# A one-layer attention and feed-forward kernel: the opening re-ordered, loads by need, both value projections moved into the first head's steps 1 and 2

## What is computed

```python
def attention(x, wq, wk, wv, wo):
    q, k, v = heads(x @ wq), heads(x @ wk), heads(x @ wv)      # 32, 8, 8 heads of 128
    q = q * cos + rotate_half(q) * sin
    k = k * cos + rotate_half(k) * sin
    scores = q @ k.T / sqrt(128), masked to keys <= query      # k, v shared by 4 query heads
    return merge(softmax(scores) @ v) @ wo

x = layernorm(x + attention(x, wq, wk, wv, wo))
nx = x * rsqrt(mean(x * x) + 1e-5) * ln_w
x = layernorm(x + (silu(nx @ gate.T) * (nx @ up.T)) @ down.T)
```

## Time and profile before

| | us |
|---|---|
| median of 3 runs | 1170.01 |
| lowest, highest run | 1169.91, 5764.48 |
| profiled execution | 1172.84 |
| its span (first to last instruction) | 1171.0 |
| PE busy | 1119.6 (96%) |
| POOL busy | 820.7 (70%) |
| DVE busy | 802.8 (69%) |
| ACT busy | 620.2 (53%) |

### The profile page before, as it was taken

How to read it: one execution, slowest core, us unless ns; L and a number is a source line. 1 busy time by engine, 2 the same in 40 slices (tenths; PEclk the granted TensorE clock), 3 DMA queues, 4 the chain that set the end, 5 groups by cost and what they waited for, 6 DMA issues and landing times.

```text
span 1171.0 us, 18940 instructions
## 1 busy us (share of the span) xinstructions
PE 1119.6 (96%) x5346; PEld 942.4 (80%) x5346; DVE 802.8 (69%) x1416; ACT 620.2 (53%) x1122; POOL 820.7 (70%) x543
## 2 busy tenths in 40 slices
PE   7799999999999999999999999999997799999997
PEld 6678888887888788878888887888775588888885
DVE  5688788778777887788788877777888742222224
ACT  4556666666666566565666566666654342212224
POOL 3489978996898789789978996898774343333431
PEclk9899999999999999999999999999999899999999
DMA  5766555555554666466555655555455301111101
GB/s 187 190 154 154 141 139 136 151 125 142 134 145 124 146 159 157 120 153 158 150 129 147 152 125 135 149 143 125 126 139 134 106 19 53 54 54 54 54 0 72
DMA packets 148346, 144.56 MB, mean 123 GB/s; under 512 B 15200, under 2 KB 128864, under 8 KB 148320
## 3 DMA queue, kind: packets, MB, share of 16 engines
q1 hardware_dynamic: 136160, 124.31, 41.3%
q10 hardware_dynamic: 12160, 19.93, 6.2%
HBM read 37.23 MB, written 2.10 MB: 34 GB/s over the span
## 4 chain that ended last, share of the span: by engine, by line
PE 62%; POOL 16%; issue 10%; DMA 4%; DVE 3%; ACT 2%; SPq 1%; ACTq 0%; POOLq 0%; DVEq 0%
PE ACC L1064 13%; PE ACC L1066 13%; PE ACC L1065 13%; PE S L1064 4%; PE S L1066 4%; PE S L1065 4%; POOL PT_lo L499 4%; POOL qk_raw L473 4%; PE S L1080 3%; PE S L1082 3%; PE S L1081 3%; POOL rope_s L474 3%; POOL Q_lo L483 2%; DMA rope_s<-qk_raw 2%; POOL wq_lo L453 2%
## 5 line engine op out<-in xcount | busy, mean ns | idle before, releaser
L803 DVE CUSTOM_DVE_ANT_0 S<-S,mask 128x128 f32<-128x128 f32 (+7 forms) x256 | 194.4, 759 | 155.0 <-PE S L1082 155.0
L593 ACT ACTIVATE probs<-S,neg_max 128x128 f32<-128x128 f32 (+7 forms) x256 | 189.2, 739 | 207.4 <-DVE neg_max L803 204.9
L499 POOL TENSOR_TENSOR PT_lo<-PT_lo,PT_hi 128x896 fp32r<-128x896 f32 (+1 forms) x97 | 218.3, 2250 | 36.2 <-ACT PT_hi L600 36.1
L814 DVE STREAM_TRANSPOSE turned<-probs 128x128 f32<-128x128 f32 (+7 forms) x256 | 197.8, 773 | 4.0 <-ACT probs L593 4.0
L874 DVE SCALAR_TENSOR_TENSOR y<-ACC,row_rcp,y 128x512 f32<-128x512 f32 x256 | 177.2, 731 | 16.6 <-PE ACC L1066 16.6
L473 POOL TENSOR_TENSOR qk_raw<-qk_raw,cos_sb 128x512 f32<-128x512 f32 x76 | 116.9, 1538 | 97.2 <-DMA rope_s<-qk_raw 97.1
L600 ACT ACTIVATE PT_hi<-PT_lo 128x896 fp32r<-128x896 f32 (+3 forms) x160 | 162.3, 1015 | 29.6 <-DMA PT_lo<-turned 29.2
L551 POOL TENSOR_TENSOR PT_lo<-rope_s,PT_hi 128x512 fp32r<-128x512 f32 x28 | 36.3, 1297 | 156.9 <-ACT PT_hi L742 156.9
L1064 PE MATMUL ACC<-PT_hi,V_hi 128*128 128x512 f32 (+3 forms) x384 | 134.2, 349 | 7.0 <-DVE PT_lo L821 4.4
L1080 PE MATMUL S<-K_hi,Q_hi 128*128 (+5 forms) x384 | 133.3, 347 | 7.4 <-ACT probs L593 5.0
L1065 PE MATMUL ACC<-PT_lo,V_hi 128*128 128x512 f32 (+3 forms) x384 | 134.9, 351 | 0.0
(11 more groups left out here) (129 smaller groups left out, 2552.0 us busy)
## 6 DMA issues: line engine op xcount, KB each, us to landing
PT_lo<-turned SPq DMA_DIRECT2D x256, 112.0 KB, 2.5
PT_lo<-turned SPq DMA_DIRECT2D x128, 208.0 KB, 4.0
rope_s<-qk_raw ACTq DMA_DIRECT2D x152, 128.0 KB, 3.8
PT_lo<-turned SPq DMA_DIRECT2D x128, 128.0 KB, 2.6
PT_lo<-turned SPq DMA_DIRECT2D x128, 80.0 KB, 2.3
wq_raw<-in_L_attn_wq_dram SPq DMA_DIRECT2D x32, 256.0 KB, 3.0
wo_raw<-in_L_attn_wo_dram SPq DMA_DIRECT2D x32, 256.0 KB, 3.7
turned<-in_L_ffn_gate_w_t_dram SPq DMA_DIRECT2D x7, 512.0 KB, 3.9
```

Source lines behind the costliest of these rows:

```text
L499: nc.gpsimd.tensor_tensor(lo, lo.bitcast(F32), hi.bitcast(F32), ALU.subtract).then_inc(pt_lo_done[half], 1)
L593: nc.scalar.activation(dst, src, ACT.Exp, bias=neg_max[:, at:at + 1], scale=-1.0, accum_out=row_sum[:, j % 2, i:i + 1]).then_inc(exp_done, 1)
L803: nc.vector.tensor_tensor_reduce(src, src, bias, scale=1.0, scalar=MASKED, op0=ALU.add, op1=ALU.min, accum_out=neg_max[:, at:at + 1]).then ...
L814: nc.vector.transpose(dst.rearrange("p b (r i) -> p r b i", i=QB), src.rearrange("p (r b i) -> p r b i", b=4, i=QB)).then_inc(turn_done, 1)
```

## The change

All of it lies in the first head and what comes ahead of it; the loops over the later heads keep their instructions.

- Both value projections leave `START` and become the extras of steps (0,1) and (0,2).
- The tables are loaded in halves: the cosine half ahead of the second half of transposed x, the sine half behind it, the two later halves after the second rotation. wk has a semaphore of its own. wv goes into `wo_raw`, issued after the first rotation, and waits for no buffer; the first wo follows it. The plain x comes in four pieces of 512 KB ahead of steps 1 to 4.
- ACT now makes the high part of wk, wv and the second wq; DVE makes the low part of wk, POOL those of wv and the second wq.
- DVE's list: key weights' low part, then a wait for both first table halves, the cosine product of q half 0, the four low parts of x's second half, and the rest of the rotations interleaved; the last two low parts and the last sum come after steps 0 and 1. ACT's list is interleaved likewise: the first copy comes ahead of the split of x's second half.
- On POOL, in steps 4 and 5 of the first head, the low part of the rotated query comes ahead of that of the probabilities.

```diff
-    if i == 0 and j + 1 < heads:
+    if j == 0 and i in V_FIRST:
+        return [V_FIRST[i] + (0, 0, NC)]
+    if i == (0 if j else 0) and j + 1 < heads:
         return [("q", 0, j + 1, 0, NC)]
...
-START = [("q", 0), ("k", 0), ("q", 1), ("k", 1), ("v", 0), ("v", 1)]
+START = [("q", 0), ("k", 0), ("q", 1), ("k", 1)]
+V_FIRST = {1: ("v", 0), 2: ("v", 1)}
...
                 if (half, begin) == (1, 0):
-                    sp.dma_start(wkv_raw[:], wk_v[:, :, 0:HD]).then_inc(wkv_in, 16)
+                    sp.dma_start(wkv_raw[:], wk_v[:, :, 0:HD]).then_inc(first_wk_in, 16)
+                    sp.dma_start(cos_sb[:, 0:HALF], cos_t[:, 0:HALF]).then_inc(table_in[0], 16)
...
-            sp.dma_start(cos_sb[:], cos_t).then_inc(cos_in, 16)
-            sp.dma_start(sin_sb[:], sin_t).then_inc(sin_in, 16)
-            sp.wait_ge(wkv_done, 1)
-            sp.dma_start(wkv_raw[:], wv_v[:, :, 0:HD]).then_inc(wkv_in, 16)
+            sp.dma_start(sin_sb[:, 0:HALF], sin_t[:, 0:HALF]).then_inc(table_in[0], 16)
...
+            rotate()
+            sp.dma_start(flat(wo_raw).rearrange("p (c n) -> p c n", n=HD), wv_v[:, :, 0:HD]).then_inc(first_wv_in, 16)
+            rotate()
+            for table, source in ((cos_sb, cos_t), (sin_sb, sin_t)):
+                sp.dma_start(table[:, HALF:T], source[:, HALF:T]).then_inc(table_in[1], 16)
+            load_wq(1)
+            rotate()
+            rotate()
             sp.wait_ge(xt_lo_done, 2 * NC)
-            sp.dma_start(y[:], x_v).then_inc(x_in, 16)
             for j, i in FIRST_HEAD:
                 if i == 1:
+                    load_wq(2)
+                if i == 0:
+                    sp.wait_ge(wkv_done, 2)
                     load_wo(0, None)
+                if i in (1, 2, 3, 4):
+                    rows = slice(i * 2 - 2, i * 2)
+                    sp.dma_start(y[:, rows, :], x_v[:, rows, :]).then_inc(x_in, 16)
...
+            for part in range(3):
+                xT_raw_high(part)
+            act_e.wait_ge(first_wk_in, 16)
+            nc.scalar.activation(wkv_hi[:], wkv_raw[:], ACT.Copy).then_inc(w_hi_done, 1)
+            copy_out("q", 0, start=True)
+            xT_raw_high(3)
+            xT_raw_high(4)
+            copy_out("k", 0, start=True)
+            start_high(0)
+            copy_out("q", 1, start=True)
+            act_e.wait_ge(first_wv_in, 16)
+            nc.scalar.activation(wo_hi[:, 1], flat(wo_raw), ACT.Copy).then_inc(w_hi_done, 1)
+            start_high(1)
+            copy_out("k", 1, start=True)
+            act_e.wait_ge(wq_in, 32)
+            nc.scalar.activation(wq_hi[:], wq_raw[:], ACT.Copy).then_inc(w_hi_done, 1)
             exponent(0, 0)
-            start_high(3, 0)
+            start_high(2)
...
             for j, i in FIRST_HEAD:
                 step(j, i, 0)
+                if i == 0:
+                    start_high(3)
...
+            xT_raw_low(0, 0, NC)
+            dve.wait_ge(w_hi_done, 2)
+            nc.vector.tensor_tensor(wkv_lo[:], wkv_raw[:], wkv_hi[:].bitcast(F32), ALU.subtract).then_inc(wkv_done, 1)
             dve.wait_ge(const_done, 7)
-            dve.wait_ge(cos_in, 16)
-            dve.wait_ge(sin_in, 16)
-            for k in range(3):
-                start_rope(k)
-            start_rope(3, meanwhile=lambda: maximum(0))
-            start_low(3)
+            dve.wait_ge(table_in[0], 32)
+            start_cos(0)
+            xT_raw_low(1, 0, NC)
+            start_sum(0)
+            start_cos(1)
+            start_low(0)
+            start_sum(1)
+            dve.wait_ge(table_in[1], 32)
+            start_cos(2)
+            start_low(1)
+            start_sum(2)
+            maximum(0)
+            start_cos(3)
...
             for j, i in FIRST_HEAD:
                 step(j, i)
-            dve.wait_ge(x_in, 16)
+                if i == 0:
+                    start_low(2)
+                    start_sum(3)
+                if i == 1:
+                    start_low(3)
+            dve.wait_ge(x_in, 16 * HT)
```

More of the change, by code:

```diff
@@ L259, in layer_kernel @@
         x_in, x_t_in = sem("x_in"), [sem(f"x_t_in{part}") for part in range(len(X_PARTS))]
-        cos_in, sin_in, ln_w_in = sem("cos_in"), sem("sin_in"), sem("ln_w_in")
+        table_in, ln_w_in = [sem(f"table_in{h}") for h in range(2)], sem("ln_w_in")
         wq_in, wkv_in, wo_in = sem("wq_in"), sem("wkv_in"), sem("wo_in")
+        first_wk_in, first_wv_in = sem("first_wk_in"), sem("first_wv_in")
         gate_in, up_in, down_in = sem("gate_in"), sem("up_in"), sem("down_in")
@@ L454, in split, with split_wq, split_wkv, split_first_wv @@
                 n.add(kind)
[L456 to L462, removed]
+            def split_wq():
+                split("wq", flat(wq_raw), flat(wq_hi), flat(wq_lo), wq_done)
+            def split_wkv():
+                split("wkv", flat(wkv_raw), flat(wkv_hi), flat(wkv_lo), wkv_done)
+            def split_first_wv():
+                split("wkv", flat(wo_raw), wo_hi[:, 1], wo_lo[:, 1], wkv_done)
             def split_wo():
                 slot = n.n["wo"] % 2
-                split("wo", flat(wo_raw), wo_hi[:, slot], wo_lo[:, slot], wo_in, wo_done)
+                split("wo", flat(wo_raw), wo_hi[:, slot], wo_lo[:, slot], wo_done)
             def rope_sum(half, ago):
@@ L504, in step @@
                     split_wo()
-                if i in (4, 5):
+                if i in (4, 5) and j > 0:
                     pt_low(i - 4)
@@ L514, in step @@
                     rope_low(*qk_halves(kind, half, head, k_slot), later)
+                if i in (4, 5) and j == 0:
+                    pt_low(i - 4)
                 if i == 6 and not (last and j >= REP - 2):
@@ L523, in _ @@
             n.add("wq")
-            split_wkv(both=True)
-            split_wkv(first=True, both=True)
+            n.add("wkv")
+            pool.wait_ge(wkv_done, 1)
+            split_first_wv()
             pool.wait_ge(x_done, 3)
-            split_wq(both=True)
-            pool.wait_ge(cos_in, 16)
-            pool.wait_ge(sin_in, 16)
+            split_wq()
+            for half in range(2):
+                pool.wait_ge(table_in[half], 32)
             pool.wait_ge(rope_lo_done, 4)
@@ L603, in weight_hi, with rope_high @@
             def weight_hi(kind, hi, raw, arrived):
-                act_e.wait_ge(arrived, n[kind] * 16 + 16)
+                act_e.wait_ge(arrived, (n[kind] - (2 if kind == "wkv" else 0)) * 16 + 16)
                 nc.scalar.activation(hi, raw, ACT.Copy).then_inc(w_hi_done, 1)
                 n.add(kind)
-            def rope_high(hi, ago=0, summed=qk_raw):
+            def rope_high(hi, ago=0):
                 act_e.wait_ge(rope_sum_done, n["rope"] - ago)
-                nc.scalar.activation(hi, summed[:, (n.n["rope"] - 1 - ago) % 2], ACT.Copy).then_inc(rope_hi_done, 1)
+                nc.scalar.activation(hi, qk_raw[:, (n.n["rope"] - 1 - ago) % 2], ACT.Copy).then_inc(rope_hi_done, 1)
             def copy_out(kind, half, start=False):
@@ L684, in _, with xT_raw_high @@
             nc.scalar.activation(wq_hi[:], wq_raw[:], ACT.Copy).then_inc(w_hi_done, 1)
-            for arrived, (half, begin, end) in zip(x_t_in, X_PARTS):
-                act_e.wait_ge(arrived, 16)
+            def xT_raw_high(part):
+                half, begin, end = X_PARTS[part]
+                act_e.wait_ge(x_t_in[part], 16)
                 for c in range(begin, end):
@@ L689, in _, with start_high @@
                     nc.scalar.activation(xT_hi[:, c, cols], xT_raw[:, c, cols], ACT.Copy).then_inc(xt_hi_done, 1)
-            def start_high(u, ago):
+            def start_high(u):
                 kind, half = START[u]
                 cols = slice(half * HALF, (half + 1) * HALF)
[L695 to L700, removed]
+                act_e.wait_ge(rope_sum_done, u + 1)
+                nc.scalar.activation(Q_hi[:, cols] if kind == "q" else K_hi[:, 0, cols], start_c[:, u % 2],
+                                     ACT.Copy).then_inc(rope_hi_done, 1)
+            for part in range(3):
[14 more added lines that the diff above has]
+            nc.scalar.activation(wq_hi[:], wq_raw[:], ACT.Copy).then_inc(w_hi_done, 1)
             exponent(0, 0)
-            start_high(3, 0)
+            start_high(2)
             n.add("wq", 2)
@@ L830, in start_low, with start_cos @@
                 nc.vector.tensor_tensor(lo, start_c[:, k % 2], hi.bitcast(F32), ALU.subtract).then_inc(rope_lo_done, 1)
-            def start_rope(k, meanwhile=None):
+            def start_cos(k):
                 half, r = START[k][1], k % 2
-                cols = slice(half * HALF, (half + 1) * HALF)
                 dve.wait_ge(copy_done, k + 1)
@@ L899, in _, with xT_raw_low @@
             nc.vector.tensor_tensor(wq_lo[:], wq_raw[:], wq_hi[:].bitcast(F32), ALU.subtract).then_inc(wq_done, 1)
-            for half in range(2):
-                for c in range(NC):
+            nc.vector.memset(eps_rms[:], RMS_EPS * LN_EPS).then_inc(y_free, ADDS_BEFORE)
```

(4 more changed lines are left out.)

26 lines of the change are left out of this document (7 added, 19 removed).

## The result

The changed kernel takes 1167.68 us (median of 9 runs, 1164.93 to 1168.83), the kernel before 1170.01 (9 runs, one of them the disturbed one). The ratio is 0.9975 with a 95% interval of 0.9965 to 0.9985: 2.9 us faster by the ratio, 2.3 by the medians, against a forecast of 2.2. The profiled execution took 1166.82 us with a span of 1165.0.

The account below looks back on a forecast made before the run. PE was taken as the bound behind 63.92 us, keeping any shift of the opening. Tile 4 of the second head at 61.7 instead of 63.92 gave 2.2 us: 1170.0 - 2.2 = 1167.8 us, range 1164.2 to 1170.4.

Parts of the forecast that it names:

- T4: Tile 4 of the second head, the opening's last wait of PE; forecast to start at 61.7 us instead of 63.92.
- The sine half, the new wait: DVE waits for the sine table's first half, landing at 14.45 us, ahead of four low parts; key-weight gain lost.
- DVE's chain to the first score: DVE's work from sine half to first score, 9.65 us; first score at 24.1 instead of 28.62, 4.5 us earlier.
- The second wq: Weights for the next query projection, split by ACT then POOL (1.26 to 1.6 us), ready at 26.2 us.
- The clock: PE's clock falls once around the next query's projection: 3.4 us at half rate, 1.7 us lost.
- Rival A: The clock doesn't fall: everything from 26.3 us is 1.7 us earlier, tile 4 at 60.0, time 1166.1; chance 0.25.
- From 26.3 to the second copy: PE works 10.3 plus 1.7 us to 38.3; then DVE, parcel and ACT put the next query's second copy at 46.4.
- From the copy to T4: Second copy of the next query to tile 4 of the second head: the same 15.2 us as before.
- C: Clock falls a second time, between row tiles' end and tile 4 of the second head: 1.7 us lost, 1169.5; chance 0.10.
- D: DVE's wait for a late sine half passes through to tile 4; landing at 18 us gives 1171.3; chance 0.08.
- E: No effect: second swap still lands at 55.1 us, late by the parcels beside it; 1170 us; chance 0.08.
- F: Larger gain: second swap and parcels land 2 to 3 us sooner, or DVE and POOL hinder less; 1164; chance 0.09.

Follow-up runs that it names:

- the run with the gap filled: Changed kernel plus five idle identity matmuls, four ahead of the first score and one behind tile 1's scores; 1166.01 us, ratio 0.9966.
- the kernel with the values alone: Kernel before with only the value projections moved to steps 1 and 2, plus ACT's third high part ahead of the first exponent; 1170.62 us, ratio 1.0003.

## Why the prediction was right

**PE as the bound behind the opening, so the shift is kept.** Right: the kernels' shifts at T4 and their times agree within 2.3 us, over a range of 9. It couldn't be had from one pair of profiles, though, as the rest scatters by 5 us.

**The number.** That 1167.7 came so close to 1167.8 is in part luck. T4 was forecast at 61.7 and came at 60.97 and 59.86, so the opening won 3.0 and 4.1 us, not 2.2; the medians were 2.3 and 3.3 below. On the way two misses of 1.1 us cancelled, as told below.

**Key weights.** k half 0 was expected at 11.5 and began at 10.78, since x and wk landed 0.5 to 0.9 sooner than in the profile of before; ended at 13.5, expected 14.4.

**The sine half, the new wait.** Expected at 14.45, it let the cosine product begin at 13.88 (12.48 in another execution). That what is won on the key weights is lost here, with q half 1 at 15.3 and k half 1 ending at 20.9 (21.2 expected), was right. Shown by the two runs that shift the wait and the one that takes it away.

**DVE's chain to the first score.** 9.65 us were summed from the table to the first score; it took 23.44 - 13.88 = 9.56, with one addition at 1.65 us beside POOL's low part of wv, as taken. The first score was at 23.44 where 24.1 was forecast, 0.57 of the 0.66 being the table's date. The reason given beside that forecast doesn't add up, though: two projections less PE's wait are 5.7 - 2.9 = 2.8 us, not 4.5. The other 1.7 are mostly PE's two waits for ACT's copies ahead of the value projections, 0.99 us at 22.15 and 0.56 at 25.77, which went with them.

**The second wq.** Expected at 26.2, ready at 25.1. POOL's operation took 1.31 us although DVE worked beside it; here DVE was the one that was held (1.64 us for its sum). I had put that price on POOL.

**The clock.** It fell, as the nearest row said and the rule of the Trainium skill, "TensorE: Matmul & The Clock Gate", "Part 1: The HAM clock gate", in its strict form, did not: PE's longest wait was 2.40 us, and 1.35 us of matmuls lay in the gap of 4.3. Rival A (0.25) is out. The run with the gap filled shows what it would have given, T4 at 57.7, not 60.0. But I mis-sized the fall, the worst term of the sum: 3.4 us at half rate were taken from the row, it was 6.8. The loss was 2.9 us at T4, not 1.7. The stretch at 1.2 GHz began at 24, ahead of the query's projection, instead of with it.

**From 26.3 to the second copy.** Tile 4's scores were to end at 38.3 and did at 38.3; the second copy was forecast at 46.4 and came at 46.29. That is closer than the terms deserve: the query's projection began at 25.2, not 26.3 (0.6 from the table, 0.5 from the second wq), and the clock took 1.1 to 1.2 more than I gave it. The work of that stretch was taken as 10.3 us, though its terms add up to 10.5; with the clock up, in the run with the gap filled, it took 10.4 (24.85 to 35.24). The parcel landed 4.4 us after its turn as taken (39.97 to 44.42).

**From the copy to T4.** 15.2 us were taken, 14.7 it was (15.0 in the other execution); row tiles at 54.69 where 54.7 was forecast.

**Rivals.** C: no second fall, the gap of 1.4 us ahead of T4 left the clock at 1.00. The wait of 2.73 us ahead of T4 in the kernel with the values alone did bring it. D: the mechanism is real, nearly every us goes through, and by my estimate from these rows the kernel would be slower than before with a table some 3 us later than 13.9; it never came near. E: out, the second swap landed at 52.20, not at 55.1, once it was issued earlier. F: in part; the swap took 4.8 us instead of 5.4.

**What I didn't see.** The move of both values bought nothing in itself. Alone it is worth 0 (1.0003), and undoing it costs the changed kernel nothing (0.9968 against 0.9976 and 0.9975, T4 2.4 to 3.6 us earlier). It opened the gap into which the clock fell; one half moved and one kept gives 0.9936 and 0.9945. The gain is that of the loads, the weight splits and the engines' order together. The plain x in pieces is worth 0.2 us of it at T4; how the rest divides among the others no run here separates.

## What to carry over

When work is moved away from in front of a wait, ask what now fills the wait: here the first score came 5.2 us earlier and 3 us arrived, since PE stood idle in the hole and then ran at half clock (2.9 us by the run with the gap filled). Follow the move to the next place where engines meet (here the second copy, held by a parcel) and price it there; the date of the first result told little (23.44 with a gain of 2.3 us, 24.53 with one of 8.2, 25.57 with none). And a wait put in front of independent work on an in-order engine, as the table wait ahead of four low parts, hands the landing date of a DMA, which varied by 1.4 us between executions, to all that follows.

## What the runs showed of the hardware that I had not expected

- After a gap the clock stayed at 1.2 GHz for 6.8 us in the changed kernel and 6.5 or more in the one with the values alone, with PE busy almost throughout (5.46 of 5.46 us); before, both falls had lasted 3.3 to 3.4 us. How long it lasts can't be taken from one row. Nor does a like stretch always bring a fall: of two executions of one kernel, with waits of 1.35 and 0.65 us in one and 1.30 and 0.67 in the other, the clock fell in the first only.
- Beside each other, DVE and POOL don't share the loss. POOL's subtraction, begun at 23.80, kept its 1.31 us while DVE's sum, begun at 24.02, took 1.64 instead of 0.69; in another place of the same trace POOL's sum, begun at 54.85, took 2.68 instead of 1.29 beside DVE's low part, begun at 54.46. In both, and at 20.34 (DVE's sum, 1.65 us, behind POOL's start at 20.16), the one that began later bore the loss, and ended 0.5 to 1.2 us after the other.
- The landing of one and the same transfer in the opening differed by 1.4 us between two executions of the same program (the operation that waits for it began at 12.48 and 13.88).
